# Rounding half of the gelu output and of the state on VectorE instead of ScalarE, with every engine's order planned anew

## The chip, the cores and the metric

The kernel runs on one core of a Trainium2 chip. The metric is the device time of one execution in microseconds (us); lower is better. A core has five engines that run side by side, each through its own queue of instructions in program order, and that wait for each other by semaphores: TensorE (PE in the profile, its weight loads PEld), VectorE (DVE), ScalarE (ACT), GpSimd (POOL) and SyncE (SP), which here only issues transfers.

## What is computed

For each of 8 batches of 1024 rows of 256 numbers: a layer norm, then the sum of the input, a linear attention block and three feed-forward blocks whose weights are stored as 4-bit codes with a low-rank addition:

```python
xn = layernorm(x)
# attention: q, k = elu(xn @ Wq + bq) + 1, the same for k; k is normalised per head; v = xn @ Wv + bv
scores = einsum('bhqd,bhkd->bhqk', q, k)
attn = einsum('bhqk,bhkd->bhqd', scores, v)
y = xn + attn @ Wo + bo                      # then a layer norm with gamma, beta
# feed-forward, h = xn, three times:
y = qlora_linear(h, qweights[2*blk], scales[2*blk], ...)
y = gelu(layernorm(y, ln_gamma[blk], ln_beta[blk]))
h = h + qlora_linear(y, qweights[2*blk + 1], ...)
return x + attention + h
```

## The kernel before

The batches run one after the other: `head()` holds the preparation of the weights and batch 0, `body(i)` is a loop over batches 1 to 6, and `tail(i)` is batch 7. There is one such triple for each engine (SyncE, GpSimd, ScalarE, VectorE, TensorE), and in each the order of the calls is written out by hand as a plan made ahead; the engine follows it to the letter. A batch is kept transposed in two column blocks (index m or k, 0 and 1, 128 of the 256 features each) and split in two halves of 512 rows (h = 0, 1). A tile is therefore 128 x 512 numbers.

Feed-forward block j (0 to 2) of half h goes through these steps:
- `first_high` and `first_low` (TensorE): the product with the first weights. To keep fp32 accuracy at the pace of fp32r, each operand is held as a high part rounded to fp32r and the rest as a low part: high weights and low weights times the high part of the state (`high_products`, L1469), then high weights times its low part (`low_products`, L1475).
- `square` (ScalarE, L620), `add_squares` (GpSimd, L417), `turn_squares` (TensorE, L1561), `ffn_var` (VectorE, L941 and L944), `ffn_root` (GpSimd, L392), `spread_rstd` (TensorE, L1569), `rb_copy` (ScalarE, L626) and `ffn_normalise` (VectorE, L953): the layer norm.
- `gelu` (ScalarE, L630), `g_higher` (ScalarE, L635), which rounds its result `fw` to `gh`, and `g_lower` (GpSimd or VectorE, L262), which takes the difference `gl`.
- `second_high` and `second_low` (TensorE, the same lines): the product with the second weights. In the last block `rows_high` (L1542) and `rows_low` (L1552) do it with the result in rows.
- `ffn_residual` (VectorE, L962): the new state `hT`; `h_higher` (ScalarE, L639) rounds it to `hTh`, and `h_lower` (GpSimd or VectorE, L267) takes the difference.

Beside this runs the attention: `project_k`, `project_q`, `k_exp` and `q_exp` (ScalarE, with a table of functions other than gelu's, hence an ACT_TABLE_LOAD at each change), `k_elu`, `k_sum`, `k_rstd` (VectorE, eleven small steps, L981 to L997), `k_hat`, `add_g`, `make_vk`, `make_m`, `attend`, then `att_y`, `ln2_root` and `att_result`. `finish` (VectorE, L1064) adds the two results; a pair of transfers stores them. For the next batch `ln1_statistics`, `ln1_mean_var` (VectorE), `ln1_root` (GpSimd), `ln1_normalise` (ScalarE), `xt` (TensorE), `xt_copy` (ScalarE) and `xt_lower` (VectorE, L1074) make the transposed input. `base_xn` (GpSimd, L412) adds the bias of the attention's output.

PSUM has eight banks: four for the feed-forward products, three that rotate through the uses in `HEAD_USES`, `BODY_USES` and `TAIL_USES`, and one for the uses in `ON_SIDE`. `take` (in TensorE's part) makes TensorE wait, before it writes a rotating bank, until the use three places earlier has been read (`read_by`). So the lists of uses and TensorE's order belong together.

The rounding of the gelu output and of the state is counted by one semaphore for each half, `g_high[h]` and `h_high[h]`, for both column blocks. In `head()`, SyncE loads the inputs in a given order (`load_x`, `load_codes`, `load_small`, `load_projection` and others), GpSimd turns codes into weights (`dequantise`: L430, then L435 with the scales), TensorE transposes them (`weight_transpose`), and `keep_busy` (L1648) is filler for TensorE while it has nothing to do.

## Time and profile before

| | |
|---|---|
| time of the runs, median (lowest to highest) | 621.18 us (621.06 to 621.93), 3 runs |
| time of the profiled execution | 621.54 us |
| its span, first to last instruction | 619.8 us |
| PE / PEld busy | 587.2 us (95%) / 499.4 us (81%) |
| DVE / ACT / POOL busy | 495.2 us (80%) / 446.1 us (72%) / 372.9 us (60%) |
| mean granted clock of TensorE | 0.998 of full speed |
| chain of waits, by engine | PE 65%, ACT 21%, DVE 6%, issue 5%, POOL 2%, DMA 1% |

"Busy" is the union of an engine's instructions. Matmuls are pipelined and their ends are modelled, so that consecutive ones overlap in the view. The chain of waits is followed back from the last instruction, at each step to what released it. "Idle before" is the time an engine stood still ahead of an instruction, with what ended it.

### The profile page before, as it was taken

The page shows a single profiled execution, that of the slowest core. Times are in us where ns is not written, and L with a number is a line of the kernel's source. Part 1 is how long each engine was busy: PE and PEld are TensorE (multiplying, and loading weights), DVE is VectorE, ACT ScalarE, POOL GpSimd, SP SyncE. Part 2 cuts the span into 40 slices and gives each one's busy share as a digit, 9 for nine tenths or more (in the row PEclk, how much of TensorE's full clock was granted, in tenths as well). Part 3 has the DMA queues.
Part 4 walks back from the last instruction along what each step waited for, and adds up shares of the span by engine and source line. Part 5 has one row for each costly group of instructions (what it writes and reads, how often), then busy time and mean ns, then how long its engine had stood idle before and what let it go on. Part 6 is the DMA issues. An engine that isn't in the chain of part 4 may idle for free.

```text
span 619.8 us, 10199 instructions
## 1 busy us (share of the span) xinstructions
PE 587.2 (95%) x3285; PEld 499.4 (81%) x3285; DVE 495.2 (80%) x1084; ACT 446.1 (72%) x699; POOL 372.9 (60%) x361
## 2 busy tenths in 40 slices
PE   4999999999998999989999999989999899999995
PEld 4787889778896889868798788968889687986885
DVE  3678789787888869797797868978697987977587
ACT  3577777859768588686787687785886957967752
POOL 4656645577454956467554684548655585646555
PEclk9999999999999999999999999999999999999999
DMA  9003000500032000500004000240004100030001
GB/s 272 29 2 136 1 0 35 171 1 1 1 119 85 0 0 0 187 16 0 0 34 169 0 0 0 79 124 0 0 0 163 40 0 0 25 111 2 0 2 69
DMA packets 11460, 29.01 MB, mean 47 GB/s; under 512 B 2592, under 2 KB 4272, under 8 KB 11440
## 3 DMA queue, kind: packets, MB, share of 16 engines
q1 hardware_dynamic: 10960, 28.35, 13.5%
q10 hardware_dynamic: 480, 0.41, 0.3%
q8 instruction: 11, 0.18, 0.1%
q14 instruction: 9, 0.07, 0.0%
HBM read 20.37 MB, written 8.39 MB: 46 GB/s over the span
## 4 chain that ended last, share of the span: by engine, by line
PE 65%; ACT 21%; DVE 6%; issue 5%; POOL 2%; DMA 1%; ACTq 0%; DVEq 0%; POOLq 0%
PE bank L1469 16%; PE bank L1596 9%; PE bank L1475 8%; PE bank L1640 6%; PE bank L1585 5%; ACT fw L630 5%; PE bank L1542 4%; PE bank L1561 3%; ACT L663 3%; ACT gh L635 3%; PE bank L1569 2%; PE bank L1552 2%; ACT hTh L639 2%; PE bank L1529 2%; PE bank L1462 2%
## 5 line engine op out<-in xcount | busy, mean ns | idle before, releaser
L262 POOL TENSOR_TENSOR gl<-fw,gh 128x512 fp32r<-128x512 f32 x80 | 103.9, 1310 | 63.1 <-ACT gh L635 62.9
L417 POOL TENSOR_TENSOR sqs<-fw 128x512 f32<-128x512 f32 x48 | 63.4, 1321 | 86.6 <-ACT fw L620 85.6
L620 ACT ACTIVATE fw<-bank,b1c 128x512 f32<-128x512 f32 x96 | 61.8, 685 | 61.0 <-PE bank L1475 61.0
L630 ACT ACTIVATE fw<-fw,vec 128x512 f32<-128x512 f32 x96 | 75.4, 808 | 7.9 <-DVE fw L953 6.8
L953 DVE SCALAR_TENSOR_TENSOR fw<-bank,b1c,rb 128x512 f32<-128x512 f32 x96 | 68.3, 745 | 10.0 <-ACT rb L626 9.9
L392 POOL TENSOR_TENSOR rsf<-vef,neghalf 128x4 f32<-128x4 f32 x48 | 52.2, 1087 | 31.1 <-DVE vef L944 29.6
L267 POOL TENSOR_TENSOR hTl<-hT,hTh 128x512 fp32r<-128x512 f32 x40 | 52.1, 1320 | 18.4 <-ACT hTh L639 18.0
L1596 PE MATMUL bank<-K,XN 128*128 128x256 f32 x256 | 62.0, 380 | 0.0
L392 POOL TENSOR_TENSOR rs<-ve,neghalf 128x2 f32<-128x2 f32 (+1 forms) x48 | 41.3, 860 | 33.6 <-DVE ve L1041 29.5
L1640 PE MATMUL bank<-M,qT 128*128 128x256 f32 x256 | 59.4, 379 | 0.0
L635 ACT ACTIVATE gh<-fw 128x512 fp32r<-128x512 f32 x96 | 56.9, 621 | 0.8
L1469 PE MATMUL bank<-gh,WTl 128*128 128x512 f32 x128 | 43.8, 423 | 10.1 <-ACT gh L635 9.9
L1640 PEld LDWEIGHTS bank<-M,qT 128*128 128x128 f32 x256 | 47.3, 190 | 6.1
L626 ACT ACTIVATE rb<-bank 128x512 f32<-128x512 f32 x48 | 28.4, 592 | 32.3 <-PE bank L1569 31.4
L1596 PEld LDWEIGHTS bank<-K,XN 128*128 128x128 f32 x256 | 46.2, 190 | 5.7 <-DVE K L1003 0.2
L941 DVE TENSOR_REDUCE bank<-bank 128x4 f32<-128x512 f32 x48 | 33.5, 699 | 15.5 <-PE bank L1561 15.0
L639 ACT ACTIVATE hTh<-hT 128x512 fp32r<-128x512 f32 x64 | 37.9, 626 | 8.0 <-DVE hT L962 7.8
L1469 PE MATMUL bank<-hTh,WTl 128*128 128x512 f32 x128 | 41.5, 406 | 0.4 <-ACT hTh L639 0.4
L962 DVE SCALAR_TENSOR_TENSOR hT<-bank,vec,hT 128x512 f32<-128x512 f32 x32 | 23.2, 747 | 22.6 <-PE bank L1475 22.6
L412 POOL TENSOR_TENSOR XNB<-XN,bo_r 128x512 f32<-128x512 f32 x32 | 40.5, 1275 | 0.0
L1469 PE MATMUL bank<-hTh,WTh 128*128 128x512 f32 x128 | 40.3, 396 | 0.0
L1469 PE MATMUL bank<-gh,WTh 128*128 128x512 f32 x128 | 40.2, 395 | 0.0
(155 smaller groups left out, 1573.0 us busy)
## 6 DMA issues: line engine op xcount, KB each, us to landing
X<-in_L_attn_x_dram SPq DMA_DIRECT2D x16, 512.0 KB, 5.8
RES<-in_L_attn_x_dram SPq DMA_DIRECT2D x16, 512.0 KB, 4.4
out_dram<-RES SPq DMA_DIRECT2D x14, 512.0 KB, 2.7
XNB<-in_L_ffn_qweights_dram SPq DMA_DIRECT2D x2, 512.0 KB, 8.2
out_dram<-RES SPq DMA_DIRECT2D x4, 256.0 KB, 2.3
RES<-in_L_ffn_qweights_dram SPq DMA_DIRECT2D x1, 512.0 KB, 9.7
Y<-in_L_ffn_lora_a_dram ACTq DMA_DIRECT2D x4, 96.0 KB, 6.5
Wp<-in_L_attn_Wk_dram SPq DMA_DIRECT2D x1, 256.0 KB, 5.9
```

The lines of the kernel that those rows point to most:

```text
L262: engine.tensor_tensor(gl[:, h, m, :], fw[:, h, m, :], gh[:, h, m, :].bitcast(F32), ALU.subtract).then_inc(g_low[h][m], 1)
L267: engine.tensor_tensor(hTl[m][:, half(h)], hT[m][:, half(h)], hTh[m][:, half(h)].bitcast(F32), ALU.subtract).then_inc(h_low[h][m], 1)
L392: return pool.tensor_tensor(dst, var, neghalf[:, 0:n], ALU.pow)
L417: pool.tensor_tensor(sqs[:, h, :], fw[:, h, 0, :], fw[:, h, 1, :], ALU.add).then_inc(sqs_ready[h], 1)
L620: act.activation(fw[:, h, m, :], FB[h][m][:], ACT.Square, bias=b1c[:, m, j:j + 1]).then_inc(sq_ready[h], 1)
L630: act.activation(fw[:, h, m, :], fw[:, h, m, :], ACT.Gelu, bias=lnb[:, m, j:j + 1], scale=lng[:, m, j:j + 1]).then_inc(g_ready[h], 1)
L635: act.activation(gh[:, h, m, :], fw[:, h, m, :], ACT.Copy).then_inc(g_high[h], 1)
L639: act.activation(hTh[m][:, half(h)], hT[m][:, half(h)], ACT.Copy).then_inc(h_high[h], 1)
L953: dve.scalar_tensor_tensor(fw[:, h, m, :], FB[h][m][:], b1c[:, m, j:j + 1], rb[:, h, :], ALU.add, ALU.mult).then_inc(yn_ready[h], 1)
L1469: pe.matmul(FB[h][m][:], w[:, l, k, m * P:(m + 1) * P], high, start=(k == 0 and n == 0), stop=False)
L1596: ins = pe.matmul(AB[:, c * D:(c + 1) * D], XN[:, t, c * P:(c + 1) * P], K[:, t, :], start=(t == 0 and c == 0), stop=(t == NT - 1), skip_g ...
L1640: ins = pe.matmul(RB[r][:, t * D:(t + 1) * D], qT[c][:, (2 * p + t) * P:(2 * p + t + 1) * P], M[:, c, :], start=(c == 0), stop=(c == NC - 1))
```

## The change

Two functions are added for VectorE, `g_higher` and `h_higher`, with the same names as ScalarE's. ScalarE keeps its own for the second column block of the gelu output and the first of the state; VectorE rounds the first column block of the gelu output and the second of the state, ten instructions of twenty in a batch. Since two engines now round, the semaphores are split by column block, and everyone who waits for them waits for that of its block. The order of the calls is changed in all three parts of all five engines, and with them the lists of uses; the set of the other calls is the same.

```diff
-        g_high, h_high = ([sem(f"{n}{h}") for h in range(2)] for n in ("g_high", "h_high"))
+        g_high, h_high = ([[sem(f"{n}{h}{m}") for m in range(NC)] for h in range(2)] for n in ("g_high", "h_high"))
...
         def g_lower(engine, i, h, j, m):
-            engine.wait_ge(g_high[h], nth(i, NBLK * NC, j * NC + m))
+            engine.wait_ge(g_high[h][m], nth(i, NBLK, j))
...
+            def g_higher(i, h, j, m):
+                dve.wait_ge(g_ready[h], nth(i, NBLK * NC, j * NC + m))
+                dve.tensor_scalar(gh[:, h, m, :], fw[:, h, m, :], 1.0, 0.0, ALU.mult, ALU.add).then_inc(g_high[h][m], 1)
+
+            def h_higher(i, h, j, m):
+                dve.wait_ge(h_ready[h], nth(i, (NBLK - 1) * NC, j * NC + m))
+                dve.tensor_scalar(hTh[m][:, half(h)], hT[m][:, half(h)], 1.0, 0.0, ALU.mult, ALU.add
+                                  ).then_inc(h_high[h][m], 1)
```

SyncE's loads in `head()`, after the change: first half of x, `lora_b` and scales, codes 0, row of `bo`, Wq, Wo, Wk, codes 1, row of `gamma`, second half of x, Wv, codes 2. Of the repeated part, the stretches that the prediction speaks of, after the change:

```diff
 # TensorE, body(i), first two thirds
+ first_high(0,0) first_low(0,0) project_k(0) project_k(1) turn_squares(0,0) first_high(1,0) first_low(1,0)
+ spread_rstd(0,0) project_k(2) project_k(3) turn_squares(1,0) project_q(0,1) spread_rstd(1,0)
+ second_high(0,0) second_low(0,0) project_q(1,0) second_high(1,0) project_q(0,0) second_low(1,0) add_g(0)
+ first_high(0,1) first_low(0,1) first_high(1,1) first_low(1,1) add_g(1) turn_squares(0,1) add_g(2..4)
+ turn_squares(1,1) spread_rstd(0,1) add_g(5..7) spread_rstd(1,1) project_q(1,1) second_high(0,1)
+ second_low(0,1) make_vk second_high(1,1) make_m second_low(1,1)
- ... project_q(0,1) spread_rstd(1,0) project_q(0,0) project_q(1,0) second_high(0,0) second_low(0,0)
- second_high(1,0) second_low(1,0) first_high(0,1) ...
 # ScalarE, body(i)
+ ... k_exp(3) gelu(0,0,0) gelu(0,0,1) rb_copy(1,0) g_higher(0,0,1) k_square(2) gelu(1,0,0) k_square(3)
+ gelu(1,0,1) g_higher(1,0,1) q_exp(0,0) h_higher(0,0,0) h_higher(1,0,0) ...
- ... k_exp(3) gelu(0,0,0) k_square(3) rb_copy(1,0) g_higher(0,0,0) gelu(1,0,0) gelu(0,0,1) g_higher(0,0,1)
- gelu(1,0,1) q_exp(0,0) g_higher(1,0,0) g_higher(1,0,1) ...
 # VectorE, body(i)
+ ... g_higher(1,0,0) k_sum(3) ffn_residual(0,0,0) k_rstd g_lower(1,0,1) k_hat(0) ffn_residual(0,0,1)
+ ffn_residual(1,0,0) h_higher(0,0,1) ffn_residual(1,0,1) q_elu(0,0) h_higher(1,0,1) ...
+ ... g_higher(1,2,0) finish(0) finish(1) xt_lower(0,1) att_y(3) att_result(2) att_result(3) finish(2)
+ finish(3) xt_lower(1,0) xt_lower(1,1)
- ... xt_lower(0,1) att_y(3) finish(0) finish(1) att_result(2) xt_lower(1,0) att_result(3) finish(2)
- xt_lower(1,1) finish(3)
 # GpSimd, body(i)
+ ... ffn_root(1,1) ln1_root(0) base_xn(1) g_lower(0,1,1) g_lower(1,1,0) g_lower(1,1,1) ...
- ... ffn_root(0,1) base_xn(1) ffn_root(1,1) base_xn(2) base_xn(3) ln1_root(0) g_lower(0,1,1) ...
 # TensorE, head()
+ keep_busy lb_transpose keep_busy x3 vec_transpose weight_transpose(0) xt(0,0) xt(0,1) qk_sums bias_mean
+ weight_transpose(2) weight_transpose(1) first_high(0,0) ...
- vec_transpose keep_busy x3 bias_mean xt(0,0) lb_transpose xt(0,1) keep_busy weight_transpose(0) qk_sums
- weight_transpose(1) first_high(0,0) ...
 # VectorE, tail(i), the end
+ ... att_y(2) g_higher(0,2,0) ffn_normalise(1,2,0) att_y(3) g_higher(1,2,0) ffn_normalise(1,2,1) finish(0)
+ att_result(2) finish(1) att_result(3) finish(2) finish(3)
```

In this listing the batch is left out of the arguments: `first_high(h, j)`, `g_higher(h, j, m)`, `xt_lower(h, c)`; `project_q(h, m)`, `project_k` and `att_y` by their part.

## Rows read from the trace of the kernel before

**Rows 1.** One window, a repeated batch: PE, PEld, DVE, ACT, POOL busy

```profile
249.41:322.47 73.06, 70.63 (x399) 60.28 (x398) 60.53 (x133) 55.02 (x87) 44.78 (x41) 1.00 0.13 43
```

**Rows 2.** Waits of PE in one repeated batch: us, times, longest

```profile
PE bank L1469 <- ACT gh L635: 1.3, 2, 1.2
PE bank L1569 <- POOL rsf L392: 0.8, 1, 0.8
PE bank L1561 <- POOL sqs L417: 0.3, 1, 0.3
```

**Rows 3.** Groups by line and shape: busy us, mean ns | idle before

```profile
L635 ACT ACTIVATE gh<-fw 128x512 fp32r<-128x512 f32 x96 | 56.9, 621 | 0.8
...
L1469 PE MATMUL bank<-hTh,WTh 128*128 128x512 f32 x128 | 40.3, 396 | 0.0
```

**Rows 4.** Chain of waits in one batch: start us, us, what

```profile
269.42 1.28 ACT L663
...
272.07 2.10 PE bank L1469 x8
...
275.11 1.87 PE bank L1469 x8
```

**Rows 5.** Single lines, VectorE: ns of one, least/median/most

```profile
L984 DVE TENSOR_SCALAR guess<-sse x8: 227/227/228, 46.5 to 562.8; 128x128 int32<-128x128 int32 x8
...
L934 DVE TENSOR_SCALAR ve<-mv x16: 170/535/1167, 6.9 to 511.8; 128x4 f32<-128x4 f32 x16
...
L262 DVE TENSOR_TENSOR gl<-fw,gh x16: 673/693/766, 51.9 to 581.8; 128x512 fp32r<-128x512 f32 x16
...
L988 DVE TENSOR_TENSOR guess_sq<-guess x24: 291/293/1381, 46.8 to 565.0; 128x128 f32<-128x128 f32 x24
```

**Rows 6.** Groups by line and shape, the layer norm's

```profile
L630 ACT ACTIVATE fw<-fw,vec 128x512 f32<-128x512 f32 x96 | 75.4, 808 | 7.9 <-DVE fw L953 6.8
L953 DVE SCALAR_TENSOR_TENSOR fw<-bank,b1c,rb 128x512 f32<-128x512 f32 x96 | 68.3, 745 | 10.0 <-ACT rb L626 9.9
L417 POOL TENSOR_TENSOR sqs<-fw 128x512 f32<-128x512 f32 x48 | 63.4, 1321 | 86.6 <-ACT fw L620 85.6
L620 ACT ACTIVATE fw<-bank,b1c 128x512 f32<-128x512 f32 x96 | 61.8, 685 | 61.0 <-PE bank L1475 61.0
```

**Rows 7.** Order of time in one batch: start us, us, instruction

```profile
261.48 0.60 PE L1561 MATMUL bank<-ident,sqs 128*128 128x128 f32 x4
...
263.09 1.02 POOL L392 TENSOR_TENSOR rsf<-vef,neghalf 128x4 f32<-128x4 f32 x1 [2.34 <-DVE vef L944]
...
264.26 0.62 PE L1569 MATMUL bank<-ident,rsf 128*128 128x128 f32 x4 [0.79 <-POOL rsf L392]
...
265.01 0.58 ACT L626 ACTIVATE rb<-bank 128x512 f32<-128x512 f32 x1
```

**Rows 8.** One window, around a batch's last block, as rows 1

```profile
300.00:326.00 26.00, 25.69 (x167) 22.91 (x166) 23.78 (x58) 18.93 (x31) 13.15 (x13) 1.00 0.05 20
```

**Rows 9.** Order of time, VectorE at the batch's turn

```profile
326.19 0.69 DVE L1064 TENSOR_TENSOR RES<-bank,RES 128x512 f32<-128x512 f32 x1
```

**Rows 10.** Order of time in the head, GpSimd and TensorE

```profile
13.28 1.06 POOL L435 TENSOR_TENSOR XNB<-XNB,sc 128x512 f32<-128x512 f32 x1 [1.61 <-DMA sc<-in_L_ffn_scales_dram]
...
15.61 0.60 PE L1730 MATMUL bank<-ident,XNB 128*128 128x128 f32 x4
...
20.94 0.82 PE L1469 MATMUL bank<-xTh,WTl 128*128 128x512 f32 x2
```

**Rows 11.** Chain of waits in the head

```profile
8.13 5.15 PE bank L1648 x24
```

**Rows 12.** The end of the chain of waits

```profile
616.60 0.69 DVE RES L1064
```

**Rows 13.** Order of time, GpSimd and VectorE at once

```profile
268.78 1.29 POOL L262 TENSOR_TENSOR gl<-fw,gh 128x512 fp32r<-128x512 f32 x1 [1.30 <-ACT gh L635]
268.83 1.38 DVE L988 TENSOR_TENSOR guess_sq<-guess 128x128 f32<-128x128 f32 x1
```

More of the change, by code:

```diff
@@ L1295, in body @@
+                g_higher(i, 1, 0, 0)
+                k_sum(i, 3)
+                ffn_residual(i, 0, 0, 0, BODY)
                 k_rstd(i)
-                ffn_residual(i, 0, 0, 0, BODY)
+                g_lower(dve, i, 1, 0, 1)
+                k_hat(i, 0)
                 ffn_residual(i, 0, 0, 1, BODY)
-                g_lower(dve, i, 1, 0, 1)
+                ffn_residual(i, 1, 0, 0, BODY)
+                h_higher(i, 0, 0, 1)
+                ffn_residual(i, 1, 0, 1, BODY)
                 q_elu(i, 0, 0, BODY)
-                ffn_residual(i, 1, 0, 0, BODY)
@@ L1741, in head @@
             def head():
-                vec_transpose()
+                keep_busy()
+                lb_transpose()
                 keep_busy()
```

554 lines of the change are left out of this document (273 added, 281 removed), and 24 rows, old and new, of tables (BODY_USES, HEAD_USES, TAIL_USES).

## The prediction

> **What bounds the kernel now.** I read the busy times by stretch first, then who TensorE waited for inside one repeated batch, then the order of time around those waits, and last the stretches in which VectorE is full. TensorE is the bound: the six repeated batches take 73.06 us each, in which it is busy 70.63 us; VectorE is busy 60.5 us, ScalarE 55.0 us, GpSimd 44.8 us [rows 1]. So ScalarE is not short of time on average, and VectorE, which takes over work, is already the fullest of the three. What can be won in a batch is TensorE's idle time, 2.43 us: 1.3 us on ScalarE's rounding of the gelu output, 0.8 us on GpSimd's root before `spread_rstd(i, 1, 0)`, 0.3 us on `add_squares` [rows 2]. A wait costs about 0.16 us more than it shows, since consecutive blocks otherwise overlap by that much in this view (a block of eight 512-column matmuls takes 1.87 us of the chain of waits, 0.234 us each, where one is shown as 0.396 [rows 3, 4]), so the stalls are some 3.3 us a batch. Over six batches and the second half of the first that is about 23 us, 4% of the kernel, and nothing in the change can win more there.
>
> **The moved rounding.** Per batch, six `g_higher(.., 0)` and four `h_higher(.., 1)` go from ScalarE to VectorE. ScalarE gives back 10 x 0.621 = 6.2 us of its 55.0 [rows 3]. VectorE's price for a 128x512 fp32 to fp32r `tensor_scalar` isn't in the trace. The nearest rows are the same instruction on 128x128 (0.227 us) and on 128x4 (0.170 us at least): a straight line through both gives 0.170 + 508 x 0.46 ns = 0.40 us. From above stands the 128x512 subtraction on VectorE, 0.693 us [rows 5]. I take 0.40, because it is the same instruction; 0.69 stays for the range. VectorE gains 10 x 0.40 = 4.0 us a batch, 64.5 of 73. That fits on average.
>
> **Gain in latency.** The wait of 1.18 us before `second_high(i, 1, 0)` exists because ScalarE does a table load (1.28 us) and a q exponential before the rounding of that block [rows 4]. With the rounding of column block 0 on VectorE, and ScalarE's q exponential planned after `g_higher(1, 0, 1)`, that wait goes: I put it at nothing. After each first gelu the rounding on VectorE also runs beside the second gelu, one 0.62 us earlier for the second column block.
>
> **What is late next.** I walked one repeated batch of the new order by hand, in each engine's new order, with durations and handoffs of the rows: 0.234 us per 512-column matmul, a square 0.685, `add_squares` 1.32, normalise 0.745, gelu 0.808 (consecutive ones start some 0.09 us before that is over) [rows 4, 6]; from the start of `turn_squares` to that of the root 1.61 us, root 1.02, spread 0.15 later, `rb_copy` 0.75 after the spread's start [rows 7]. TensorE then stalls (the cost to the chain, overlap included):
> - `turn_squares(0, 0)`: 0.4. Its bank is freed by `xt_lower(1, 1)` of the batch before, which is now VectorE's very last step. See below.
> - `spread_rstd(1, 0)`: 1.05, as before (0.79 and the 0.16): one `project_q` still stands between the turn and the spread, and variance and root take 2.6 us from the turn on.
> - `second_high(0, 0)`: 0.7. Before, 2.8 us of `project_q` stood in front of it; now it follows the spread directly, and ScalarE still has two gelus, `rb_copy(1, 0)` and a rounding to do behind its table load.
> - `first_high(0, 1)`: 0.4, for the second state block, rounded on VectorE behind `k_hat(0)` and two residuals.
> - smaller ones before `add_g(2)` 0.15, `spread_rstd(1, 1)` 0.25, `second_low(0, 1)` 0.4 (GpSimd now does `ln1_root` and `base_xn(1)` ahead of that `g_lower`) and `turn_squares(0, 2)` 0.5, as before (0.31 and 0.16).
>
> Together 3.85 us, against some 3.6 now (the 2.43 idle, four times 0.16, and about half a microsecond of small steps): +0.25, which I round up to +0.3 us a batch for the extra port waits below. Seven batches' worth is +2.1 us. The gain of 1.3 us at `second_high(1, 0)` is real in this sum; it is handed back in pieces of 0.3 to 0.7 us.
>
> **VectorE at the end of a batch.** In the 26 us around the last block VectorE is busy 23.78 us, and it runs without a pause into the next batch, where its last `finish` starts at 326.19, 3.7 us after TensorE began that batch at 322.47 [rows 8, 9]. The change adds two roundings here (0.8 us) and moves both `xt_lower(1, ..)` behind both `finish`es. By the walk the last one ends 6.0 us into the next batch, where before even that `finish` had begun at 3.7, and `turn_squares(0, 0)`, planned 5.7 us in, needs its bank. This is where the 0.4 us comes from and the place with the least room.
>
> **Head and tail.** Before, TensorE's first `high_products` starts at 20.94. Its weights wait for the scales, which SyncE loads seventh, after both halves of x, and which let GpSimd multiply only at 13.28 [rows 10]. In the new order the scales and codes come straight behind the first half of x. TensorE's filler then limits: three `keep_busy` (5.15 us [rows 11]) now stand between `lb_transpose` and everything else. With `lora_b` landing near 7.3, half a microsecond before the 7.8 at which the last small vector let TensorE begin, the first weight transposition, before at 15.61, comes near 12.6. What stood between it and `high_products` took 5.3 us; three small blocks (0.4 us each, the 0.62 shown for `spread_rstd` in rows 7 less the overlap) and one more weight transposition (an estimate of 1.3, a quarter of the 5.3) are added, so `high_products` lands near 20.4 with one transposition more already done: 0.5 + 1.3, -1.8. From below -3; from above +1, since the second half of x now lands behind nine transfers. In the tail the chain of waits ends on VectorE, whose last `finish` starts at 616.60 [rows 12]. The new tail has `att_result(3)` done ahead of the last two `finish`es, but puts two roundings (0.8 us) into a queue that is full from `att_y(0)` on, and `rows_high` waits for the first of them, which stands behind `att_y(2)`. I put +0.7, between 0 and +2.
> Sum: +2.1 - 1.8 + 0.7 = +1.0 us. The profiled execution of before took 621.54 us (span 619.8), 0.36 above the median of 621.18. On the median: 622.2.
>
> **The rule that speaks against the change.** In the trace VectorE waits when GpSimd is running. A square of 128x128 that began 0.05 us behind GpSimd's subtraction of 268.78 took 1.38 us [rows 13], where the shortest took 0.291; a `tensor_scalar` on 128x4 takes from 0.170 to 1.167 us, half of them over 0.535 [rows 5]. The moved roundings are of the second kind, and GpSimd is busy 61% of a batch [rows 1]. The Trainium skill ("SBUF — State Buffer", section "Who interferes with whom") calls this an exclusive lock on a port pair that VectorE's two-port modes and GpSimd share, held for the whole instruction, and counts `tensor_scalar` among them; by that rule, each of the ten roundings may wait for a whole GpSimd instruction and GpSimd for each of them, and the trace agrees with its 1.38 us.
>
> **The rivals.**
> - Port waits pile up (slower). If six in ten roundings wait half of the 1.29 us of a GpSimd subtraction [rows 13], VectorE gains another 3.9 us a batch. Four roundings have TensorE right behind them. This decides where VectorE's lag at `turn_squares(0, 0)` exceeds the 5.7 us: the end phase has 26 - 23.8 = 2.2 us left, 0.8 is used by the roundings, so from about 0.7 us of waiting per rounding on it is lost. Price +1.0 us a batch on the forecast, 7 in all: 629. For it: [rows 5, 13]. Against: GpSimd is idle at several of the ten by my walk.
> - The new order fits better than my walk (faster). Five of my eight stalls are 0.4 us or less, and half a microsecond of earlier ScalarE removes each. If they and half of `second_high(0, 0)` go, 1.3 us a batch is won, less with a neighbour taking over: 1.2 x 7 = 8.4 below the forecast, 613.8. For it: ScalarE's 6.2 us. Against: what TensorE waits for most is the variance chain over VectorE, GpSimd and back, which the change doesn't shorten.
> - The rounding costs 0.69 us, as the subtraction does (slower). Three of TensorE's waits grow by 0.29: 0.9 x 7 = 6 us, 628. No row of that size speaks for it; the 128x128 row speaks against.
>
> **How the numbers follow.** Forecast 622.2, with its own range 619 to 625.5: 0.40. Better fit 613.8: 0.27. Port waits 629: 0.25. Slow rounding 628: 0.08. This kernel's measurement can tell 0.2%, 1.24 us, from no change: 619.9 to 622.4. The forecast's own case splits 0.07 faster, 0.22 same, 0.11 slower; of port waits 0.02 may end as same. Faster 0.34, same 0.24, slower 0.42. The range leaves out the lower part of the better fit (0.12) and the upper part of the port waits (0.07): 612.5 to 630.
>
> **What would show it.** In one repeated batch of the changed kernel: `second_high(1, 0)` without a wait; a wait of 0.5 to 0.8 us before `second_high(0, 0)`; the rounding on VectorE at about 0.40 us at its shortest, with a maximum near 1.6; VectorE near 65 us busy of 73.3; the batch at 73.0 to 73.6 us. The first `high_products` at 20 to 21 us. The prediction is wrong if the batch leaves that window by more than 0.5 us, or if the head moves by more than 3.

## The result and the profile after

The changed kernel takes 616.8 us (median; 616.49 to 617.46) where the kernel before takes 621.12 (620.77 to 621.93): ratio 0.993, 95% interval 0.9913 to 0.9947. It is 0.7% faster. The forecast was 622.2, so the direction was missed; the time lies inside the range. The profiled execution has a span of 615.2 us against 619.8.

The first part of the page of the changed kernel, and its chain of waits by engine:

```profile
PE 590.7 (96%) x3285; PEld 498.3 (81%) x3285; DVE 526.9 (86%) x1164; ACT 402.8 (65%) x619; POOL 373.9 (61%) x361
...
PE 70%; ACT 9%; POOL 7%; DVE 6%; issue 6%; DMA 1%; ACTq 1%; DVEq 0%; POOLq 0%
```

One repeated batch of it, in the columns of [rows 1], and TensorE's waits in it, as [rows 2]:

```profile
394.63:467.09 72.46, 71.19 (x397) 60.09 (x396) 63.88 (x142) 49.70 (x77) 44.45 (x41) 1.00 0.13 43
```

```profile
PE bank L1578 <- POOL rsf L392: 0.8, 1, 0.8
PE bank L1570 <- POOL sqs L417: 0.3, 1, 0.3
PE bank L1478 <- DVE gh L937: 0.2, 1, 0.2
```

A repeated batch takes 72.44 us (72.21 for the first) instead of 73.06 [rows 1]. VectorE's busy time rose by 3.35 us a batch and ScalarE's fell by 5.3. The ten roundings took 5.6 us of VectorE in this batch, so the rest of its work took some 2.2 us less, 1.3 of them in `k_rstd` (below). TensorE's idle time fell from 2.43 to 1.27 us; the 1.3 us on ScalarE's rounding [rows 2] has shrunk to 0.2 us on VectorE's. The two waits on GpSimd are what they were.

To split the 4.6 us of span I take two points where both kernels have just finished the last `rows_low` of a batch. In the order of time TensorE starts the next block, in the changed kernel, at:

```profile
102.29 0.64 PE L1478 MATMUL bank<-xTh,WTl 128*128 128x512 f32 x2
...
536.73 0.62 PE L1478 MATMUL bank<-xTh,WTl 128*128 128x512 f32 x2
```

In the kernel before the same points lie at:

```profile
103.13 0.40 PE L1585 MATMUL bank<-Wqkl,xTh 128*128 128x256 f32 x2
...
541.49 0.40 PE L1585 MATMUL bank<-Wqkl,xTh 128*128 128x256 f32 x2
```

So the head gave 0.84 us, the six repeated batches 438.36 - 434.44 = 3.9 us, and the tail lost 0.1 (78.4 against 78.3 us). The body is the finding, and the place where the forecast (+2.1) went wrong.

The moved instruction on VectorE, single lines as in [rows 5] (`g_higher`, `h_higher`, and for comparison a layer norm step whose first source is a bank):

```profile
L937 DVE TENSOR_SCALAR gh<-fw x48: 416/427/571, 41.7 to 605.1; 128x512 fp32r<-128x512 f32 x48
...
L941 DVE TENSOR_SCALAR hTh<-hT x32: 411/606/1346, 54.1 to 589.3; 128x512 fp32r<-128x512 f32 x32
...
L923 DVE SCALAR_TENSOR_TENSOR fw<-bank,b1c,rb x96: 733/743/753, 38.0 to 605.5; 128x512 f32<-128x512 f32 x96
```

### The profile page after: what moved, and what is told of

The parts are those of the page before. It is cut to its first block, busy times and chain, and to the rows that moved or that the text cites. A ratio compares the mean times of both kernels' runs of the same rounds, so it can differ in the third digit from the quotient of the medians.

```text
span 615.2 us, 10218 instructions
## 1 busy us (share of the span) xinstructions
PE 590.7 (96%) x3285; PEld 498.3 (81%) x3285; DVE 526.9 (86%) x1164; ACT 402.8 (65%) x619; POOL 373.9 (61%) x361
## 4 chain that ended last, share of the span: by engine, by line
PE 70%; ACT 9%; POOL 7%; DVE 6%; issue 6%; DMA 1%; ACTq 1%; DVEq 0%; POOLq 0%
PE bank L1478 19%; PE bank L1484 9%; PE bank L1594 7%; PE bank L1605 7%; PE bank L1649 6%; PE bank L1551 4%; PE bank L1616 4%; PE bank L1570 3%; ACT fw L630 3%; POOL gl L262 2%; ACT L630 2%; PE bank L1578 2%; PE bank L1561 2%; PE bank L1538 2%; PE bank L1471 2%
## 5 line engine op out<-in xcount | busy, mean ns | idle before, releaser
L267 POOL TENSOR_TENSOR hTl<-hT,hTh 128x512 fp32r<-128x512 f32 x40 | 54.1, 1368 | 39.8 <-ACT hTh L639 33.0
L392 POOL TENSOR_TENSOR rsf<-vef,neghalf 128x4 f32<-128x4 f32 x48 | 50.6, 1055 | 43.7 <-DVE vef L914 43.0
L1478 PE MATMUL bank<-gh,WTl 128*128 128x512 f32 x128 | 42.5, 412 | 1.4 <-DVE gh L937 1.4
L1478 PE MATMUL bank<-hTh,WTl 128*128 128x512 f32 x128 | 43.1, 418 | 0.0
L601 ACT ACTIVATE xTh<-bank 128x512 fp32r<-128x512 f32 x32 | 19.2, 599 | 35.8 <-PE bank L1471 35.7
L1484 PE MATMUL bank<-gl,WTh 128*128 128x512 f32 x128 | 36.9, 410 | 0.0
L1578 PE MATMUL bank<-ident,rsf 128*128 128x128 f32 x192 | 29.0, 274 | 6.8 <-POOL rsf L392 6.8
```

What stands on the lines that cost most here:

```text
L267: engine.tensor_tensor(hTl[m][:, half(h)], hT[m][:, half(h)], hTh[m][:, half(h)].bitcast(F32), ALU.subtract).then_inc(h_low[h][m], 1)
L392: return pool.tensor_tensor(dst, var, neghalf[:, 0:n], ALU.pow)
L1478: pe.matmul(FB[h][m][:], w[:, l, k, m * P:(m + 1) * P], high, start=(k == 0 and n == 0), stop=False)
L1484: ins = pe.matmul(FB[h][m][:], WTh[:, l, k, m * P:(m + 1) * P], low, start=False, stop=(k == NC - 1))
```

## The experiments

All numbers are medians; each ratio is to the kernel before, run on the same chip. "Batch" is the distance of two repeated batches in the profiled execution. The runs come from several series, and the median of the kernel before differs between these by up to 0.8 us (621.1 to 621.9). So where two kernels of different series are compared, the batch is the surer measure.

| kernel | us | ratio (95%) | batch, us |
|---|---|---|---|
| before | 621.1 to 621.9 | 1 | 73.06 |
| changed | 616.8 | 0.993 (0.9913 to 0.9947) | 72.44 |
| a1 order of three ScalarE steps | 624.0 | 1.0037 (1.0023 to 1.0052) | 73.48 |
| a2 engine only | 649.7 | 1.0456 (1.0434 to 1.0479) | 78.1 |
| a3 order only | 634.6 | 1.0211 (1.0188 to 1.0234) | 75.23 |
| a4 changed, old tail | 616.75 | 0.9918 (0.9901 to 0.9934) | 72.43 |
| a5 changed, old head | 618.5 | 0.995 (0.9936 to 0.9963) | 72.44 |
| b1 a1, k_rstd moved | 646.4 | 1.0401 (1.0381 to 1.0422) | 77.0 |
| b2 a2, k_rstd moved | 656.3 | 1.0555 (1.0541 to 1.057) | 78.8 |
| b4 changed, project_q moved | 617.15 | 0.9925 (0.9911 to 0.9938) | 72.53 |
| c3 changed, one GpSimd step moved | 621.7 | 1.0001 (0.9988 to 1.0014) | 73.2 |
| c4 b4, k_rstd late | 632.5 | 1.0156 (1.0133 to 1.0178) | 74.68 |
| c5 b4, a Newton step less | 612.2 | 0.9846 (0.9829 to 0.9863) | 71.65 |
| c6 changed, slow rounding | 634.2 | 1.0195 (1.018 to 1.0211) | 74.70 |
| d1 c4, k_rstd in two parts | 637.6 | 1.0259 (1.0245 to 1.0273) | 75.84 |
| d2 d1, one rounding back | 637.0 | 1.0246 (1.0232 to 1.026) | 75.8 |
| d3 changed, a Newton step less | 616.6 | 0.9922 (0.9909 to 0.9936) | 72.44 |
| e1 c4, two roundings back | 627.8 | 1.0101 (1.0085 to 1.0116) | 74.25 |
| e2 a1, a Newton step less | 618.7 | 0.995 (0.9936 to 0.9963) | 72.5 |

### Order or engine? a1, a2, a3

a1, in ScalarE's `body` of the kernel before:

```
 gelu(i, 1, 0, 1)
-q_exp(i, 0, 0, BODY)
 g_higher(i, 1, 0, 0)
 g_higher(i, 1, 0, 1)
+q_exp(i, 0, 0, BODY)
```

> The kernel before with one change, in ScalarE's order of the repeated batch: g_higher(i, 1, 0, 0) and g_higher(i, 1, 0, 1) run ahead of q_exp(i, 0, 0) and its table load instead of behind it. Nothing goes to VectorE. Theory A (the whole gain of the changed kernel's body is the removed wait of second_high(i, 1, 0), and the place of the rounding in the order is enough for it): the 1.34 us that TensorE loses there goes, 1.0 to 1.3 us a batch, six batches, 613.5 to 615 against 621.1. Rival B (the two roundings and the q exponential compete for the same time of ScalarE, so the exponential's late end shows up at a later wait, and only the other engine helps): less than 0.4 us a batch, 619 to 621.

Measured: 624.0 us, slower than both theories allowed. The wait at `second_high(i, 1, 0)` is gone, and TensorE waits 1.56 us one block later, at `second_low(i, 1, 0)`. The order of time in a1:

```profile
270.15 2.59 POOL L262 TENSOR_TENSOR gl<-fw,gh 128x512 fp32r<-128x512 f32 x2 [1.30 <-ACT gh L635]
270.21 1.38 DVE L988 TENSOR_TENSOR guess_sq<-guess 128x128 f32<-128x128 f32 x1
...
271.62 1.26 DVE L990 SCALAR_TENSOR_TENSOR guess_off<-guess_sq,sse 128x128 f32<-128x128 f32 x1
...
275.43 0.68 DVE L262 TENSOR_TENSOR gl<-fw,gh 128x512 fp32r<-128x512 f32 x1
...
276.16 0.19 PEld L1475 LDWEIGHTS bank<-gl,WTh 128*128 128x128 f32 x1 [2.00 <-DVE gl L262]
276.16 0.51 PE L1475 MATMUL bank<-gl,WTh 128*128 128x512 f32 x1 [1.56 <-ACT hTh L639]
```

Read it from below. The product of the low parts needs VectorE's `g_lower(i, 1, 0, 1)`, which ends at 276.11; the load of its weights names it. (The matmul's own row names ScalarE's rounding of the state, whose result no product of `gl` reads: a releaser is the last semaphore event, not always the one needed.) That `g_lower` stands behind the eleven small steps of `k_rstd`, and two of these, 0.29 us by themselves, took 1.38 and 1.26 us while GpSimd ran two `g_lower` in a row. Such a lengthening of a VectorE instruction beside one of GpSimd is called a port wait below. In the kernel before only one of the 0.29 us steps was hit [rows 13]: GpSimd's next `g_lower` waited for ScalarE's late rounding until `k_rstd` was over. The earlier rounding on ScalarE made GpSimd earlier, and GpSimd made VectorE later. So a1's gain was handed back with interest.

a2 keeps the orders of the kernel before and moves the ten roundings alone; VectorE's `body`, cut:

```
 k_sum(i, 2)
+g_higher(i, 0, 0, 0)
...
+g_higher(i, 1, 0, 0)
 k_rstd(i)
...
 ffn_residual(i, 0, 0, 1, BODY)
+h_higher(i, 0, 0, 1)
...
```

> The kernel before with its orders kept; only the ten moved roundings of a repeated batch run on VectorE, each set behind the instruction of VectorE that in the changed kernel too runs at about that time. Head and tail still round on ScalarE. Theory A (moving the engine takes away the 1.34 us at second_high(i, 1, 0), and TensorE, whose order is before's, keeps its 2.8 us of project_q ahead of second_high(i, 0, 0), so nothing new gets late): 0.8 to 1.2 us a batch, 614 to 616.5. Rival B (VectorE without a new plan has no room at the end of the batch, and its port waits pile up there): turn_squares(i, 0, 0) gets late, 620 to 625.

a3 keeps the orders of the changed kernel and puts the ten back:

```
 gelu(i, 0, 0, 0)
+g_higher(i, 0, 0, 0)
...
 h_higher(i, 0, 0, 0)
+h_higher(i, 0, 0, 1)
...
```

> The changed kernel with all its orders; only the ten roundings of a repeated batch go back to ScalarE, each right behind its gelu (state: right behind the rounding of the other column block). Theory A (in the new order second_high(i, 0, 0) follows spread_rstd(i, 1, 0) directly, so it needs the rounding off ScalarE's queue): TensorE waits 0.6 to 1.2 us longer there and 0.3 us at some of the other three second_high, 6 to 10 us in all, 622 to 627. Rival B (the gain was the new order alone, the engine is indifferent): 616 to 618.

Measured: 649.7 and 634.6 us. Each half of the change by itself is a loss, 5.0 and 2.2 us a batch; only both together give -0.6. For a2 this holds with the roundings at the places chosen here; other places were not tried. Rival B was right in sign, but far too small (620 to 625) and wrong in the place: `turn_squares(i, 0, 0)` does not wait for VectorE. TensorE's longest wait in one batch of a2, VectorE's `g_lower` that it waits for, and two stretches around it (columns as in [rows 1]):

```profile
PE bank L1484 <- DVE gl L262: 3.0, 1, 3.0
...
```

```profile
207.56 1.75 DVE L262 TENSOR_TENSOR gl<-fw,gh 128x512 fp32r<-128x512 f32 x1
```

```profile
205.90:210.90 5.00, 1.99 (x8) 1.25 (x8) 4.97 (x7) 1.53 (x3) 3.20 (x2) 0.99 0.00 0
210.90:213.90 3.00, 3.00 (x8) 2.31 (x7) 2.96 (x8) 0.41 (x1) 2.51 (x2) 0.50 0.00 0
```

It is the place of a1 again: `second_low(i, 1, 0)` waits 3.0 us for VectorE's `g_lower`, ahead of which `k_rstd` with two port waits, two residuals and a rounding now stand, and which itself takes 1.75 us instead of 0.69 while GpSimd runs `h_lower`. And the wait costs more than itself: TensorE's granted clock is 0.50 in the stretch that follows (1.2 of 2.4 GHz), where consecutive matmuls are 0.425 us apart instead of 0.234. One of the six batches prices this: there the wait is the same 3.0 us, the clock stays at full speed, and the batch takes 76.7 us instead of 78.1, 1.4 us less.

In a3 the waits are ScalarE's:

```profile
PE bank L1570 <- POOL sqs L417: 1.0, 1, 1.0
PE bank L1478 <- ACT gh L635: 0.8, 2, 0.4
PE bank L1578 <- POOL rsf L392: 0.8, 1, 0.8
PE bank L1484 <- DVE gl L262: 0.5, 1, 0.5
PE bank L1551 <- ACT gh L635: 0.4, 1, 0.4
```

So theory A was right in its cause (the new order needs the roundings off ScalarE) and too small: 2.8 us a batch over the changed kernel where I had 1 to 1.7, 634.6 us where I had 622 to 627. The cost is spread over five places, one of them `add_squares` of the last block, 0.7 us later.

### Head and tail: a4, a5

a4 and a5 take the orders of the last batch, or of the first one with its loads, from the kernel before, and leave the rest of the changed kernel.

> The changed kernel with the last batch in the orders of the kernel before (its roundings on ScalarE), head and repeated batches unchanged. Theory A (from the start of the last batch to the end the changed kernel takes 79.6 us and the kernel before 78.15, and that is the tail's own order): 1.4 us less than the changed kernel, 615.4. Rival B (the tail is longer because the body hands it over in another state, VectorE's last xt_lower 5.9 us late into it): no gain or a loss, 616.8 to 618.

> The changed kernel with the first batch, loads and preparation of the weights in the orders of the kernel before (its roundings on ScalarE); repeated batches and tail unchanged. Theory A (the head's own order is worth the 0.84 us by which its end comes earlier in the changed kernel, in spite of the 0.21 at the first high_products): 617.6, 0.8 us above the changed kernel. Rival B (the head's gain is only what the first repeated batch finds ready, or the 0.21 us of the first matmul): 616.8 to 617.0.

Measured: 616.75 and 618.5 us. The tail is worth nothing either way. The 1.4 us that I had read there came from comparing unlike points: the changed kernel starts a batch with another block, and at the points used above the difference is 0.1. a5 lies above both theories (617.6; 616.8 to 617.0). Against the changed kernel it loses 1.7 us in the medians and 1.4 us in its trace, where the first repeated batch starts at 103.65 instead of 102.29; against the kernel before the new head is worth 0.84. Most of the difference of 0.5 comes from the join: TensorE starts the last `rows_low` of the head at 102.35 in a5 and 102.19 in the kernel before, but the new body opens with `first_high`, for which a5 has to wait (0.20 us idle), while the old body opens with a projection.

### Can `k_rstd` get out of the way? b1, b2

In both, VectorE's `body`:

```
-k_rstd(i)
 ffn_residual(i, 0, 0, 0, BODY)
 ...
 g_lower(dve, i, 1, 0, 1)
+k_rstd(i)
```

> a1_two_roundings_earlier with one more move, in VectorE's order of the repeated batch: the eleven small steps of k_rstd(i) run behind g_lower(i, 1, 0, 1) instead of ahead of the two residuals before it. Still no rounding on VectorE. In a1 the wait did not go, it moved: TensorE waited 1.56 us at second_low(i, 1, 0) for that g_lower, which stood behind k_rstd on VectorE, where two of the small steps took 1.26 and 1.38 us beside GpSimd's g_lower. Theory A (the gain of the changed kernel's body is the taking away of both waits, ScalarE's and VectorE's, and both can be had by order alone): 1.2 to 1.5 us a batch under before's 73.06, 612 to 615. Rival B (VectorE has to do k_rstd somewhere, and behind g_lower it makes q_elu, the residuals of half 1 and k_hat late, which TensorE then meets at first_high(i, 1, 1) or add_g): 618 to 622.

> a2_engine_only with the same one move: k_rstd(i) behind g_lower(i, 1, 0, 1) on VectorE. In a2 TensorE waited 3.01 us at second_low(i, 1, 0) for that g_lower, and its next eight matmuls came 0.425 us apart instead of 0.234. Theory A (nearly all of a2's 5.0 us a batch is that one wait with the slower matmuls behind it): the batch comes back to 72.0 to 73.3, 613 to 622. Rival B (VectorE with ten roundings in the old order is late at many places): 74.5 us a batch or more, over 628.

Measured: 646.4 and 656.3 us. b1 lies far over both theories, theory A's sharpest miss; b2 lies in rival B's range, but by one wait of 3.6 us at the same place as in b1, not by many. TensorE's longest wait in one batch of b1:

```profile
PE bank L1469 <- ACT hTh L639: 3.1, 1, 3.1
...
```

The wait at `second_low` is gone and 3.1 us stand at `first_high(i, 1, 1)`, again with slower matmuls behind. What I had left out: in the kernel before `k_rstd` fills a hole. Without it VectorE is idle for 3.5 us until TensorE has finished `second_low(i, 0, 0)`, and then does `k_rstd` with two port waits (5.4 us) in front of the residuals of half 1. Its place was not the error; it cost nothing there.

### One limit or two? b4, c5, d3

b4, TensorE's `body` of the changed kernel (and the order of the banks with it):

```
 project_q(i, 0, 1, BODY)
+project_q(i, 1, 0, BODY)
 spread_rstd(i, 1, 0, BODY)
 second_high(i, 0, 0, BODY)
 second_low(i, 0, 0)
-project_q(i, 1, 0, BODY)
 second_high(i, 1, 0, BODY)
```

> The changed kernel with one block of TensorE moved in the repeated batch: project_q(i, 1, 0) runs ahead of spread_rstd(i, 1, 0) instead of behind second_low(i, 0, 0). Its 1.4 us then cover the root that TensorE waits 0.77 us for (0.94 lost) and the 0.34 lost at second_high(i, 0, 0). Theory A (the wait for the variance chain is short of cover only): 0.7 to 1.1 us a batch less, 610 to 613. Rival B (second_high(i, 1, 0), which has lost the 1.4 us in front of it, waits for ScalarE's rounding of column block 1 instead, and takes the gain): 615.5 to 617.5.

Measured: 617.15 us, no gain; rival B's number, but not its mechanism. TensorE's longest wait in one batch:

```profile
PE bank L1479 <- DVE gl L257: 0.9, 1, 0.9
...
```

The wait of 0.8 before `spread_rstd(i, 1, 0)` [rows 2] is gone, and 0.9 has appeared at `second_low(i, 1, 0)`, for VectorE's `g_lower` once more. (The edits shift the lines: L1479 here is L1484 of the changed kernel.) c5 is b4, and d3 the changed kernel, with a shorter `k_rstd`:

```
-NEWTON = 3
+NEWTON = 2
```

> b4_q_ahead_of_spread with two Newton steps instead of three in k_rstd of every batch: this leaves out the third step, three small instructions of VectorE of 0.29 us, 0.98 us with their handoffs; the root of the key norm is less exact. Theory A (b4's wait at second_low(i, 1, 0) is the length of k_rstd in front of VectorE's g_lower): that wait falls from 0.92 to nothing, the batch from 72.53 to 71.5 to 71.8, 611 to 613. Rival B (the wait is set by ScalarE's rounding of column block 1 ahead of g_lower, or TensorE then waits at first_high(i, 0, 1)): under 0.3 us a batch, 615.5 to 617.

> The changed kernel with two Newton steps instead of three in k_rstd of every batch (the third is left out, 0.98 us of VectorE), and project_q where the changed kernel has it. b4 (project_q moved, three steps) gave no gain, c5 (moved, two steps) 0.87 us a batch. Theory A (two equally late limits stand side by side: the root that spread_rstd(i, 1, 0) waits for, and VectorE's queue with k_rstd ahead of g_lower; either removed alone gives nothing): less than 0.2 us a batch under 72.44, 615.3 to 616.8. Rival B (VectorE's queue alone is the limit): 0.6 us a batch or more, 613 or less.

Measured: c5 612.2 us, d3 616.6, both as theory A said. TensorE's waits in one batch of c5, and two of the four of d3, with the rounding of the state that the second one names:

```profile
PE bank L1565 <- POOL sqs L412: 0.3, 1, 0.3
PE bank L1473 <- ACT gh L630: 0.3, 1, 0.3
```

```profile
PE bank L1578 <- POOL rsf L392: 0.8, 1, 0.8
...
PE bank L1478 <- DVE hTh L941: 0.2, 1, 0.2
```

```profile
416.91 1.48 DVE L941 TENSOR_SCALAR hTh<-hT 128x512 fp32r<-128x512 f32 x1
```

The four kernels make a square. Move `project_q`: 0. Shorten `k_rstd` by 0.98 us: 0. Both: 0.8 us a batch, 4.6 us in all. There are two limits of nearly the same length in this stretch: the variance chain that ends in GpSimd's root, and VectorE's queue from the layer norm over `k_rstd` to `g_lower(i, 1, 0, 1)`. TensorE shows a wait only for the one that comes first in its order; the other shows none and is just in time. One corner of the square is not clean: in d3 that rounding starts 0.09 us behind GpSimd's `h_lower` and takes 1.48 us, against 0.79 in the changed kernel and 0.69 in c5. So part of d3's 0.98 us is lost again on VectorE itself; how much of its zero is this port wait and how much the variance chain was not separated. In the changed kernel:

```profile
410.94 1.31 POOL L262 TENSOR_TENSOR gl<-fw,gh 128x512 fp32r<-128x512 f32 x1 [0.56 <-DVE gh L937]
...
412.05 0.28 DVE L960 TENSOR_SCALAR sse<-ss 128x128 f32<-128x128 f32 x1
...
415.24 0.29 DVE L976 SCALAR_TENSOR_TENSOR rk<-guess_off,guess 128x128 f32<-128x128 f32 x1
...
415.45 0.68 DVE L262 TENSOR_TENSOR gl<-fw,gh 128x512 fp32r<-128x512 f32 x1
...
415.71 1.20 PE L1484 MATMUL bank<-gl,WTh 128*128 128x512 f32 x4
...
417.20 1.29 POOL L267 TENSOR_TENSOR hTl<-hT,hTh 128x512 fp32r<-128x512 f32 x1 [4.95 <-ACT hTh L639]
```

`g_lower` ends at 416.13, and the four matmuls of `second_low`, the later two of which need it, run from 415.71 with next to no gap (1.20 us, where an undisturbed four take 1.09 to 1.10).

### What the new order really gained: c3

The same rows show what is new: `k_rstd` runs from 412.05 to 415.53, 3.48 us, without one port wait, because GpSimd is idle beside it from 412.25 to 417.20. In the kernel before it took 4.79 us, with the one port wait of [rows 13] and a first step of 0.51 us instead of 0.28. GpSimd's last `g_lower` of this stretch ends 10.2 us after the start of the root of [rows 7] in the kernel before, and 6.3 us after it in the changed kernel (405.95 to 412.25); `k_rstd`, which starts 2.1 us later than before, begins when GpSimd is nearly done.

That is the work of the order, not of the engine that rounds. In a3, where ScalarE does all the roundings, the root starts at 266.55, GpSimd's last `g_lower` ends 7.0 us later, and `k_rstd` starts behind it and takes 3.42 us, again without a port wait, in all six batches:

```profile
272.25 1.30 POOL L262 TENSOR_TENSOR gl<-fw,gh 128x512 fp32r<-128x512 f32 x1 [0.59 <-ACT gh L635]
...
273.98 0.22 DVE L970 TENSOR_SCALAR sse<-ss 128x128 f32<-128x128 f32 x1
```

What the moved roundings add is that the same chain comes earlier: VectorE's `g_lower` ends 11.46 us after the root's start in a3 and 10.19 us after it in the changed kernel. c3 takes the port-free stretch away again, in GpSimd's `body` of the changed kernel:

```
-base_xn(i, 0, BODY)
 ffn_root(i, 1, 0)
 ...
 g_lower(pool, i, 1, 0, 0)
+base_xn(i, 0, BODY)
```

> The changed kernel with one instruction of GpSimd moved in the repeated batch: base_xn(i, 0) (1.29 us) runs behind g_lower(i, 1, 0, 0) instead of ahead of the root, so that it lies beside VectorE's k_rstd, where GpSimd was idle for 4.9 us. Theory A (k_rstd, which took 3.4 us without one port wait in the changed kernel and 4.7 us with one of 1.38 in the kernel before, stands in front of the g_lower that second_low(i, 1, 0) needs, and the free stretch beside it is part of the gain): k_rstd takes 1.0 us more or twice that, and the batch 0.7 to 1.3 us more, 621 to 625. Rival B (the port wait is absorbed by the project_q in front of second_low(i, 1, 0), and GpSimd's place is indifferent): 616.5 to 617.5.

Measured: 621.7 us, ratio 1.0001 (0.9988 to 1.0014). One GpSimd instruction in the wrong place undoes the whole change. The order of time in c3:

```profile
415.58 1.29 POOL L412 TENSOR_TENSOR XNB<-XN,bo_r 128x512 f32<-128x512 f32 x1
415.74 1.21 DVE L963 TENSOR_SCALAR guess<-sse 128x128 int32<-128x128 int32 x1
...
419.81 0.68 DVE L262 TENSOR_TENSOR gl<-fw,gh 128x512 fp32r<-128x512 f32 x1
...
420.54 0.74 PE L1484 MATMUL bank<-gl,WTh 128*128 128x512 f32 x2 [0.83 <-DVE gl L262]
```

One step takes 1.21 instead of 0.23 us, `g_lower` ends 0.98 later, TensorE waits 0.83 for it, and the batch is 0.75 longer, 4.9 us in all. From the root's start to the end of that `g_lower` it is 10.75 us in the kernel before, 10.19 in the changed one and 11.16 in c3. The difference of the first two, 0.56, is near the 0.62 by which their batches differ, but that proves nothing: in the kernel before this `g_lower` ended 0.64 us before TensorE needed it. It ended there at 273.84:

```profile
273.08 0.77 DVE L262 TENSOR_TENSOR gl<-fw,gh 128x512 fp32r<-128x512 f32 x1
```

The Trainium skill ("SBUF — State Buffer", section "Who interferes with whom") says that VectorE instructions with two inputs in SBUF, and those forms that use both its ports, shut GpSimd out and are shut out by it for a whole instruction, while one with a single SBUF input outside those forms is not. The traces agree: the steps of `k_rstd` take up to 1.38 us beside GpSimd, and 96 layer norm steps whose first source is a bank stay between 733 and 753 ns.

### Moving `k_rstd` once more: c4, d1, d2, e1

c4, on top of b4 (VectorE; on TensorE `add_g(i, 0)` goes behind `first_low(i, 1, 1)`):

```
 ffn_residual(i, 0, 0, 0, BODY)
+g_lower(dve, i, 1, 0, 1)
+ffn_residual(i, 0, 0, 1, BODY)
+h_higher(i, 0, 0, 1)
 k_rstd(i)
 ...
 h_higher(i, 1, 0, 1)
+k_hat(i, 0)
```

> b4_q_ahead_of_spread with VectorE's queue opened: g_lower(i, 1, 0, 1), ffn_residual(i, 0, 0, 1) and h_higher(i, 0, 0, 1) run ahead of k_rstd, both residuals of half 1 right behind it, and k_hat(i, 0) behind h_higher(i, 1, 0, 1); on TensorE add_g(i, 0) goes behind first_low(i, 1, 1). In b4 the 1.28 us taken away before spread and second_high(i, 0, 0) came back as 1.08 at second_low(i, 1, 0) and 0.1 to 0.3 elsewhere. Theory A (TensorE is held in this stretch by VectorE's queue, and k_rstd, 3.4 us that nobody needs before add_g, is what stands in it): second_low(i, 1, 0) without a wait, 0.7 to 1.1 us a batch under b4, 610 to 613. Rival B (k_rstd now lies beside GpSimd's h_lower, waits for the port, and the late residuals of half 1 hold first_high(i, 1, 1), as in b1): 618 or more.

d1 cuts it, d2 and e1 return roundings of the state to ScalarE:

```
 k_rstd_begin(i)                    # eight steps
 ffn_residual(i, 1, 0, 0, BODY)
 ffn_residual(i, 1, 0, 1, BODY)
 h_higher(i, 1, 0, 1)
 q_elu(i, 0, 0, BODY)
 newton_step(i, NEWTON - 1)         # three steps
 k_hat(i, 0)
```

> c4_k_rstd_late with k_rstd cut in two: its first eight small steps stand where it stood, then come both residuals of half 1, h_higher(i, 1, 0, 1) and q_elu(i, 0, 0), then the last three steps and k_hat(i, 0), and the statistics of the next batch's x behind k_hat(i, 1) and k_hat(i, 2). In c4 the first eight steps ran without a port wait, and the last three took 2.8 us beside GpSimd's h_lower, ahead of residuals that TensorE then waited 1.31 us for at first_high(i, 1, 1). Theory A (only that order inside VectorE's queue spoiled c4): 1.3 to 2.0 us a batch under c4's 74.68, with 0.3 to 0.6 us left at first_high(i, 0, 1); 72.4 to 73.2 a batch, 616 to 621. If VectorE's later steps meet no new wait of TensorE, 71.6, 611.5. Rival B (VectorE is the bound of the whole stretch up to add_g, so what is put later is waited for later, at add_g(i, 0) or the squares of half 1): 74 a batch or more, 626 and up.

> d1_k_rstd_in_two_parts with one rounding of the repeated batch back on ScalarE, h_higher(i, 1, 0, 1), right behind h_higher(i, 1, 0, 0), where ScalarE was idle for 3.9 us in c4. Theory A (in this stretch VectorE's queue is the bound and ScalarE has room): 0.3 to 0.5 us a batch less than d1. Rival B (TensorE does not wait for VectorE's last steps): within 0.1 us a batch of d1.

> c4_k_rstd_late (k_rstd whole, behind g_lower(i, 1, 0, 1) and ffn_residual(i, 0, 0, 1)) with h_higher(i, 0, 0, 1) and h_higher(i, 1, 0, 1) back on ScalarE, which was idle there, and q_elu(i, 0, 1), k_hat(i, 1) and k_hat(i, 2) ahead of the second set of statistics. k_rstd then starts 0.4 us earlier and meets one GpSimd instruction instead of two. Theory A (k_rstd is harmless where GpSimd is quiet and nothing of TensorE's stands behind it): the 1.31 and 0.56 at first_high(i, 1, 1) go, about 72.1 to 72.6 a batch, 614.5 to 618. Rival B (the steps that run beside h_lower cost 0.98 each whatever their number, and k_hat and q_elu get late for TensorE): 74 a batch or more, 626 and up.

Measured: 632.5, 637.6, 637.0 and 627.8 us; rival B each time, in d2 with 0.04 us a batch less than d1. (Two of c4's six batches take 1.2 us more than the 74.68 of the others; see the last section.) Each frees `second_low(i, 1, 0)` and pays elsewhere. In d1 the last three steps fall beside GpSimd's `h_lower` and `add_squares`, and each of them is hit:

```profile
433.32 0.79 DVE L965 TENSOR_TENSOR guess_sq<-guess 128x128 f32<-128x128 f32 x1
...
434.14 1.26 DVE L967 SCALAR_TENSOR_TENSOR guess_off<-guess_sq,sse 128x128 f32<-128x128 f32 x1
...
435.44 1.25 DVE L974 SCALAR_TENSOR_TENSOR rk<-guess_off,guess 128x128 f32<-128x128 f32 x1
```

```profile
PE bank L1608 <- DVE K L984: 1.4, 1, 1.4
PE bank L1573 <- DVE qT L991: 1.3, 1, 1.3
```

3.3 us for three steps of 0.29, and the waits (the two rows above, one batch of d1) move on to `add_g(i, 0)` and to the squares of half 1, whose bank a `q_elu` frees too late. e1 ran `k_rstd` with two waits of that kind and left 1.3 us at the first products of the state. The five us in which GpSimd is idle are the only good place for these eleven steps that I found, and the changed kernel has them there. None of the kernels with the whole computation beats the changed kernel: a4 equals it.

### The same limit in the kernel before: e2

e2 is a1 with `NEWTON = 2`.

> a1_two_roundings_earlier with two Newton steps instead of three in k_rstd of every batch (the third is left out, 0.98 us of VectorE). Theory A (in the orders of the kernel before, too, VectorE's queue with k_rstd in it is the limit that stands right behind ScalarE's late rounding): TensorE's wait at second_low(i, 1, 0) falls from 1.56 to about 0.6, the batch from 73.48 to about 72.5, 616 to 618. Rival B (another wait takes its place): 73 or more a batch, 620 or more.

Measured: 618.7 us, 0.7 above theory A's range, and 72.5 a batch, as theory A said: the wait at `second_low(i, 1, 0)` falls from 1.56 to 0.6. With the rounding on ScalarE and all other orders old, 0.98 us less in VectorE's queue gives back 0.98 us a batch and lands on the batch of the changed kernel. So in the kernel before, too, VectorE's queue stood right behind ScalarE's late rounding.

### The price of a longer rounding: c6

```
-dve.tensor_scalar(gh[:, h, m, :], fw[:, h, m, :], 1.0, 0.0, ALU.mult, ALU.add)
+dve.tensor_tensor(gh[:, h, m, :], fw[:, h, m, :], fw[:, h, m, :], ALU.max)
```

and the same for `hTh`.

> The changed kernel with VectorE's moved roundings written as the maximum of the tile with itself, a tensor_tensor with two inputs, which takes 0.68 to 0.69 us on this shape where tensor_scalar took 0.42. Ten in a batch, 2.6 us more of VectorE. Theory A (VectorE's queue holds TensorE in the first stretch of the batch, where two roundings of g stand ahead of k_rstd and g_lower, and at the second products): 0.5 to 1.0 us a batch and as much in head and tail, 620 to 624. Rival B (the rounding's length is covered at most of its ten places): under 0.3 us a batch, 616.8 to 618.5. The prediction priced this at 6 us in all.

Measured: 634.2 us, far over both theories. The roundings took 0.69 us (state: 0.85 in the middle), VectorE 67.8 us a batch instead of 63.9, and the batch 74.70: 13.5 us over the six, 2.9 ahead of them, 1.5 in the tail.

## Why the prediction missed

- **What bounds the kernel, and the moved rounding**: right. TensorE is the bound; the rounding takes 0.41 us at its shortest and 1.35 at its longest (0.40 and 1.6 forecast), VectorE is at 63.9 us a batch (65 forecast). The port waits were placed wrong: the six roundings of g have hardly any (0.427 in the middle, 0.571 at most), the four of the state 0.3 us each on average.
- **Gain in latency**: right in its effect, incomplete in its cause. `second_high(i, 1, 0)` waits no more. But a1 shows that this wait was not worth 1.3 us: behind it stood VectorE's queue. In the kernel before VectorE's `g_lower` ends at 273.84, only 0.64 us ahead of the matmul that needs it (274.48), so with nothing else changed 0.6 us was all there was to win.
- **What is late next**: this step failed. Eight stalls of together 3.85 us were added up. Found were (idle time and 0.16): 0.16 at `turn_squares(0, 0)` for 0.4, 0.94 before the spread for 1.05, 0.34 and 0.15 in `second_high(0, 0)` for 0.7, 0.12 for 0.4 at `first_high(0, 1)`, 0.47 for 0.5 at `turn_squares(0, 2)`, and nothing at the three others for 0.8: 2.2 us in place of 3.85. Every term was too big or as big. A walk errs by a few tenths at each place in both directions, but a stall cannot be negative, so only the errors towards late enter such a sum; and waits on one chain are not independent: b4, c5 and d3 show that removing one of them can be worth nothing, and a late start at one place covers the next. The comparison base was too high as well: 3.6 where the same list gives 3.2 for the kernel before (0.95, 0.31, 1.34, 0.47, 0.13). So the stalls fell by 1.0 us a batch where they were forecast to grow by 0.25. And one cost of 0.5 us was in none of the terms (last paragraph of this section).
- **The port waits**: the rule was known and had its row [rows 13], but I used it in one direction only, as 0.3 us a batch of extra cost. The new order removes a port wait of 1.1 us (1.38 for 0.29) from `k_rstd`, ahead of the one instruction that is just in time. I had that very wait in my rows and did not ask whether the new order still had it. c3 prices a port wait there at 4.9 us, the whole result.
- **VectorE at the end of a batch**: right in the timing (the last `xt_lower` ends 5.7 us into the next batch, 6.0 forecast), and too dear: 0.01 us idle at `turn_squares(0, 0)`.
- **Head and tail**: the first `high_products` starts at 20.73 (20.4 forecast, 20.94 before). The head gave 0.84 us by the marks, where 1.8 was forecast; the tail cost 0.1 where 0.7 was. These two errors (0.96 and 0.6) nearly cancel, by luck, so the miss of the whole is about that of the body: -3.9 where +2.1 was forecast. That the time fell inside the range is no merit either: the range reached that far down for the better fit, whose cause is not the one found.
- **Rivals**: the better fit (613.8) had the right sign and named ScalarE's earlier end as its cause; that is a3 against the changed kernel, and holds only together with GpSimd's new place. Port waits that pile up are real (a1, a2, d1), but in the changed kernel they are fewer on the whole: VectorE is only 3.35 us a batch busier for ten roundings of together 5.6. The slow rounding was priced at 6 us and costs 17.4: the step that failed is "three of TensorE's waits grow by 0.29"; the rounding's 0.27 a piece grew to 3.9 us of VectorE a batch, port waits with it, and 2.26 of these arrived at TensorE.
- **What would show it**: of the six signs, the wait before `second_high(i, 0, 0)` (0.5 to 0.8 forecast, 0.18 found) and the batch (73.0 to 73.6 forecast, 72.44 found, 0.56 under it) spoke against the prediction, the latter by its own bound.

That the longer batch of a2, a3 and c4 to e1 comes only from the places named was read from their rows, not tested one by one. TensorE's idle time fell by 1.16 us and the batch only by 0.62, since its busy time rose from 70.63 to 71.19 us with the same matmuls. From start to start this can be placed. From `spread_rstd(i, 1, 0)` to `second_low(i, 1, 0)`, with the same work between, TensorE takes 9.75 us in the kernel before (264.26 to 274.01) and 8.60 in the changed one (407.11 to 415.71). From there to `first_low(i, 0, 1)` it takes 2.80 us before (274.01 to 276.81) and 4.15 after (415.71 to 419.86), of which 0.86 are the four matmuls of `add_g(i, 0)` that the new order has there: 0.5 us more. The rest of the batch is equal within 0.04. In that stretch three weight loads of the changed kernel wait for VectorE, for `g_lower`, for `k_hat` and for the second rounding of the state, and none does in the kernel before:

```profile
416.19 0.30 PEld L1484 LDWEIGHTS bank<-gl,WTh 128*128 128x128 f32 x2 [0.28 <-DVE gl L262]
416.79 0.73 PEld L1605 LDWEIGHTS bank<-K,XN 128*128 128x128 f32 x4 [0.30 <-DVE K L982]
...
418.82 0.30 PEld L1478 LDWEIGHTS bank<-hTh,WTl 128*128 128x128 f32 x2 [0.40 <-DVE hTh L941]
```

Each is too short to show as idle time, since the matmuls around it overlap in this view. Read so, VectorE's queue takes back nearly half of what the new plan gains ahead of it. A shorter `k_rstd` does not return it: the same stretch takes 4.15 us in d3 and 4.13 in c5. What would was not tested.

## What to carry to other kernels

Before pricing the removal of a wait, look for what is just in time behind it: follow the other operands of the next two blocks to the ends of their queues and subtract. In a planned order VectorE's serial small steps belong where GpSimd is quiet, since each of them can be hit once per GpSimd instruction (here a step of 0.29 us took up to 1.38); read a new order for what lies beside such a chain, not only for what lies ahead of a wait. And do not add up small stalls from a walk: take the largest lateness on each chain, and see whether the next one is already covered by it.
